# Start-up of a four-part layer kernel: loads from two engines, and batch 0's first steps placed among the set-up

## The chip, the cores and the metric

The kernel runs on one core of one Trainium2 chip. The metric is the device time of one execution in microseconds (us); lower is better. A core has five engines that each run their own list of instructions: PE (matmul, transposes), DVE (vector), ACT (activation), POOL (GpSimd) and SP (here it issues DMAs and nothing else). They meet at semaphores only. Sixteen DMA engines move the data.

## The reference

The input is x of 16 batches by 512 tokens by 128 features, float32. Four blocks follow each other, each closed by a norm:

1. RWKV: `x1 = LN(x)*g0 + b0`; `xn = LN(x1)`; three mixes `xn*mix + shift(xn)*(1-mix)`, where `shift` moves by one token; k, v, r by 128x512 matrices; two recurrences over the tokens, `s = k + decay*s`, where `decay = exp(-exp(tm_decay))`; read-out, residual, then a channel mix (two mixes, silu, sigmoid gate).
2. A soft tree of depth 8: sigmoid gates of `(x Wq) routers^T`, 256 leaf probabilities, times leaf values, times `Wout`, plus a bias.
3. Causal attention of 16 heads of 8 dimensions with rotary positions, after an RMS norm.
4. A mixture of 16 experts with the two best kept, and two shared experts.

Weights are used in forms that the kernel makes itself: `Wq` and the routers are fused, the leaves and `Wout` are fused, the expert matrices are transposed, and the rotary matrices are laid out by dimension.

## The kernel before, in words

**Set-up.** SP issues batch 0's load of x, then 41 loads of weights and vectors in one loop over the list LOADS (L312), every one of them adding to the one semaphore "loaded". The ten short vectors (`pre_g` to `norm_scale`, 128 numbers each, one column of the tile `vec` each) are last in the list. POOL meanwhile fills constants (L326), among them `kh` (75 rows of 8192, the key heads' tile with rows of ones), and makes the identity and the masks (L331). Then every engine waits for the whole of "loaded" (`ALL_LOADED`):

- DVE scales weights (L576 to L581), lays out `w_rope` (L586 to L588), makes the products of vectors `now_g`, `before_g` (L592 to L597), splits the expert biases (`brow_part`, L603 to L613) and the shared bias (`bias_part`, L617 to L629), and, after the fused matmuls, finishes `w_leaf` (L631, L633), which counts "leafed".
- PE waits for "loaded", "scaled", "rot" and "brow_parts", then turns 23 matrices (TURNS: routers, leaves, `wout`, centroids, shared and 16 expert matrices, L852) through the PSUM banks, bank n mod 8, and does the fused matmuls (L855, L857). Before its first batch step it waits for "leafed" and for the bias rows.
- ACT makes `decay` and `first` (L445 to L448), copies each turned matrix out of its bank (L452), and the fused results (L454, L456).
- SP waits for the bias parts, issues three small loads of `bias_rows` (L315), and starts its batch steps.

**Batches.** After the set-up each engine runs the order written out by hand in ORDER. A token `1:mix1` is step mix1 of the batch that lies one turn back. `run` goes through 16 turns and the lags behind; in one turn several batches are at work in different blocks. The first steps of a batch form one chain: `moments0` (DVE, L643 and L648) of x0, `root0` (POOL, L341 to L349), `norm0` (ACT, L469), `x1_gain` and `x1_bias` (POOL, L366, L370), `moments1` (DVE), `root1` (POOL), `norm1` (ACT) into `hat`, `xnT` (PE, L867, four transposes into T0, which is bank 0), `mix_before0` to 2 (ACT, L463), `mix0` to 2 (DVE, L652) into `mixed`, and then `k0` (PE, L871), the first matmul with `wk`, which waits for all three mixes. The DVE order of the next turn begins with mix1, mix2 and `moments0` of the next batch, then `clamp0`. In SP's order, step `load` in turn 0 loads x of batch 1.

The shortest statement of what orders a turn (L276 to L279):

```python
for turn in range(B + max(lag for lag, _ in order)):
    for lag, name in order:
        if 0 <= turn - lag < B:
            steps[name](turn - lag)
```

Of the kernel before, what the change touches and what calls it, by code (L numbers as in the profile page):

```python
# [21 lines left out]
DH = 8  # L22
# [71 lines left out]
def build(nc: bass.Bass, a, out):  # L94
    with ExitStack() as ctx:
        def sb(name, shape, dt=F32):
# [4 lines left out]
                 ("loaded", "brow_parts", "zeroed", "ident", "scaled", "decay1", "decay", "turned_ps", "turned", "fused_ps", "fused", "leafed",  # L101
# [131 lines left out]
        def value_columns(j, g, q):  # L233
# [5 lines left out]

        LOADS = [  # L240
# [6 lines left out]
            (g0[:, :], a["L0_attn_ln0_g"].rearrange("(o h) -> o h", o=1).broadcast_to([P, P])),  # L247
            (b0[:, :], a["L0_attn_ln0_b"].rearrange("(o h) -> o h", o=1).broadcast_to([P, P])),
# [24 lines left out]
        def run(engine, steps):  # L273
# [13 lines left out]
        def _(sp):  # L287
# [33 lines left out]
        def _(pool):  # L321
            zeroed = (ident[:, :], identb[:, :], maskb[:, :], maskTb[:, :], vaug[:, :], ksum[:, :, 0:1], kvsum[:, 0:1],
                      gT[:, :], owner[:, :], brow_part[:, :, :], bias_rows[:, :], max_cols[:, :], gate_cols[:, :])
            filled = ((exponent[:, :], -0.5), (minus_one[:, :], -1.0), (eps_ln[:, :], LN_EPS), (keps[:, :], K_EPS), (kh[:, :, :], 1.0), (ones_rows[:, :], 1.0))
# [106 lines left out]
            pool.wait_ge(setup["loaded"], ALL_LOADED)  # L431
            run("pool", {
# [5 lines left out]
            })  # L438
# [3 lines left out]
        def _(act):  # L442
            act.wait_ge(setup["loaded"], ALL_LOADED)
            act.wait_ge(setup["ident"], 6)
            act.activation(dec_e[:, :], tdec[:, :], ACT.Exp).then_inc(setup["decay1"], 1)  # L445
            act.activation(first[:, :], tfirst[:, :], ACT.Exp).then_inc(setup["decay1"], 1)
            act.wait_ge(setup["decay1"], 2)
            act.activation(decay[:, :], dec_e[:, :], ACT.Exp, scale=-1.0).then_inc(setup["decay"], 1)  # L448

            for n, (_, rows, dst) in enumerate(TURNS):  # L450
                act.wait_ge(setup["turned_ps"], n + 1)
                act.activation(dst, bank[n % 8][:, 0:rows], ACT.Copy).then_inc(setup["turned"], 1)  # L452
            act.wait_ge(setup["fused_ps"], 1)
# [724 lines left out]
```

## Time and profile before

| | |
|---|---|
| median of 3 runs | 1983.46 us (1978.99 to 1986.34) |
| the profiled execution's own time | 1981.15 us |
| its span in the trace | 1979.4 us |
| busy share of the span: PE, DVE, ACT, POOL | 84%, 77%, 51%, 46% |
| granted TensorE clock, mean over the span | 0.944 of full |

The profile is of one execution. Its span runs from the first to the last instruction. "PE" is a matmul's time, "PEld" a weight load, "SPq" the SP queue that issues DMAs. PEclk is the TensorE clock that was granted, as a share of full speed (1.00 is 2.4 GHz, 0.50 is 1.2 GHz). A line such as L643 is that of the kernel's source.

### The profile page before, as it was taken

Reading aid. Unit: us, or ns where it says so; the run is one execution under the profiler, and the core shown is the slowest. Engines: PE = TensorE matmul, PEld = TensorE weight load, DVE = VectorE, ACT = ScalarE, POOL = GpSimd, SP = SyncE. Lnnn points to the kernel's source line nnn. Section 1 sums busy time; section 2 is a strip of 40 time slices with the busy share of each in tenths; the row PEclk is TensorE's granted clock in tenths of the full one; section 3 lists DMA queues with packets and bytes.
Section 4 is the critical chain, followed back from the end, with each engine's and each line's share of the span. In section 5 each row is a group of like instructions: output and inputs, shape, how many; then the busy total and the mean of one; then the engine's idle time right before and its main releaser. Section 6 shows DMA issues by size and latency. Waiting matters only on the chain.

```text
span 1979.4 us, 33699 instructions
## 1 busy us (share of the span) xinstructions
PE 1664.5 (84%) x12063; PEld 1082.8 (55%) x12141; DVE 1526.5 (77%) x3386; ACT 1005.9 (51%) x1997; POOL 914.3 (46%) x1117
## 2 busy tenths in 40 slices
PE   1365799989898999989898989989898989988785
PEld 1133456565565656565565656565665657564535
DVE  2756879889797979889797979789797969783712
ACT  1232374655646374655556474746556464736252
POOL 3436253635545363635455364636355463622202
PEclk9677899999999999999999999999999999999887
DMA  3001010010101010010101010100101010100000
GB/s 97 0 6 48 7 39 17 8 54 8 54 8 49 7 54 6 24 37 8 54 7 49 7 54 7 37 25 8 54 8 54 2 54 2 45 11 25 31 7 6
DMA packets 64617, 53.35 MB, mean 27 GB/s; under 512 B 6018, under 2 KB 63170, under 8 KB 64450
## 3 DMA queue, kind: packets, MB, share of 16 engines
q1 hardware_dynamic: 64450, 51.19, 8.4%
q8 instruction: 97, 1.59, 0.4%
q14 instruction: 70, 0.57, 0.1%
HBM read 8.44 MB, written 4.19 MB: 6 GB/s over the span
## 4 chain that ended last, share of the span: by engine, by line
PE 42%; DVE 36%; issue 6%; ACT 5%; SPq 5%; POOL 3%; DMA 3%; DVEq 0%; ACTq 0%; POOLq 0%
PE bank L871 40%; DVE rmax L742 12%; SPq L300 4%; DVE rmax L739 3%; DVE wkb L689 3%; ACT prob L463 3%; DVE prob L822 3%; PE bank L867 3%; DMA kh<-part 2%; DVE stats L643 2%; DVE tree L652 1%; DVE kvsum L681 1%; DVE kk L665 1%; SPq L312 1%; DVE ksum L676 1%
## 5 line engine op out<-in xcount | busy, mean ns | idle before, releaser
L463 ACT ACTIVATE prob<-bank 128x512 f32<-128x512 f32 x640 | 359.4, 600 | 85.6 <-PE bank L871 80.1
L742 DVE TENSOR_REDUCE rmax<-bank 128x1 f32<-128x512 f32 (+2 forms) x768 | 353.4, 504 | 29.6 <-PE bank L871 29.1
L871 PE MATMUL bank<-kh,qh 72*128 72x512 bf16 (+3 forms) x1024 | 259.8, 308 | 52.8 <-DVE rmax L742 38.1
L871 PE MATMUL bank<-qh,kh 75*128 75x512 bf16 (+3 forms) x1024 | 257.4, 306 | 24.7 <-ACT prob L463 20.8
L871 PE MATMUL bank<-wexpT,prob 128*128 128x128 f32 x2048 | 271.7, 280 | 2.1 <-POOL prob L429 0.6
L871 PEld LDWEIGHTS bank<-wexpT,prob 128*128 128x128 f32 x2048 | 258.7, 195 | 21.0 <-issue 15.9
L429 POOL TENSOR_TENSOR prob<-xdT,spread 128x512 f32<-128x512 f32 x128 | 173.6, 1356 | 193.5 <-ACT spread L463 193.4
L463 ACT ACTIVATE spread<-bank 128x512 f32<-128x512 f32 x128 | 76.5, 597 | 298.1 <-PE bank L871 251.1
L871 PEld LDWEIGHTS bank<-qh,kh 75*128 75x128 bf16 x1024 | 100.1, 98 | 205.4 <-ACT prob L463 146.0
L689 DVE RECIPROCAL wkb<-wkb 128x512 f32<-128x512 f32 x64 | 211.6, 3326 | 0.0
L871 PE MATMUL bank<-maskb,identb 128*128 128x128 bf16 x1024 | 194.3, 223 | 0.0
L871 PE MATMUL bank<-maskTb,identb 128*128 128x128 bf16 x1024 | 192.9, 221 | 0.0
L871 PEld LDWEIGHTS bank<-kh,qh 72*128 72x128 bf16 x1024 | 102.1, 100 | 140.0 <-DVE rmax L742 78.7
L871 PE MATMUL bank<-prob,vaug 128*32 128x512 f32 (+3 forms) x2048 | 173.9, 446 | 0.0
L341 POOL TENSOR_TENSOR var<-mv,eps_ln 128x4 f32<-128x4 f32 x112 | 27.8, 248 | 271.3 <-DVE mv L648 270.6
L463 ACT ACTIVATE rth<-bank 128x512 f32<-128x512 f32 x128 | 75.1, 592 | 150.7 <-PE bank L871 137.3
L375 POOL TENSOR_TENSOR wkb<-wkb,ksum 128x512 f32<-128x512 f32 x64 | 77.2, 1213 | 129.8 <-DVE ksum L676 117.7
L871 PE MATMUL bank<-mixed,cwk 128*128 128x512 f32 x128 | 87.8, 803 | 43.4 <-DVE mixed L652 43.4
L871 PEld LDWEIGHTS bank<-maskb,identb 128*128 128x128 bf16 x1024 | 102.6, 100 | 37.8 <-issue 25.7
L871 PEld LDWEIGHTS bank<-maskTb,identb 128*128 128x128 bf16 x1024 | 101.4, 99 | 25.8 <-issue 25.0
L384 POOL TENSOR_TENSOR rth<-rth,kvb 128x512 f32<-128x512 f32 x64 | 96.9, 1515 | 39.2 <-DVE kvb L652 39.2
L345 POOL TENSOR_TENSOR rstd<-var,exponent 128x4 f32<-128x4 f32 x112 | 113.6, 1014 | 1.2
(209 smaller groups left out, 3401.6 us busy)
## 6 DMA issues: line engine op xcount, KB each, us to landing
qh<-part SPq DMA_DIRECT2D x144, 128.0 KB
kh<-part SPq DMA_DIRECT2D x144, 128.0 KB
x<-in_L_attn_x_dram SPq DMA_DIRECT2D x16, 256.0 KB, 2.9
out_dram<-yo SPq DMA_DIRECT2D x16, 256.0 KB, 2.3
qh<-maxT SPq DMA_DIRECT2D x16, 48.0 KB
wk<-in_L_attn_tm_Wk_dram SPq DMA_DIRECT2D x1, 256.0 KB
wv<-in_L_attn_tm_Wv_dram SPq DMA_DIRECT2D x1, 256.0 KB
wr<-in_L_attn_tm_Wr_dram SPq DMA_DIRECT2D x1, 256.0 KB
```

Source lines behind the costliest of these rows:

```text
L300: sp.dma_start(dst[r:KROWS:PARTS * PARTS, :, :], part[t][m][:, :]).then_inc(sems["heads_in"], 16)
L345: raised(pool.tensor_tensor(rstd[:, n, :], var[:, n, :], exponent[:, :], ALU.pow), f"root{n}")
L375: raised(pool.tensor_tensor(wkb[:, c % 2, :], wkb[:, c % 2, :], ksum[:, c % 2, 0:T], ALU.add), "wk")
L384: raised(pool.tensor_tensor(rth[:, c % 2, :], rth[:, c % 2, :], kvb[:, c % 2, :], ALU.mult), "gated")
L429: raised(pool.tensor_tensor(ug[:, e % 4, :], xdT[:, :], spread[e // 2 % 2][:, :], ALU.mult), "ug_side")
L463: raised(act.activation(dst, src, func, **kw), signal)
L689: raised(dve.reciprocal(wkb[:, c % 2, :], wkb[:, c % 2, :]), "wk_inv")
L739: last = dve.tensor_reduce(rmax[:, 1, h:h + 2], S[n % 2].rearrange("p (h s) -> p h s", h=2), AX_X, ALU.max)
L742: last = dve.tensor_reduce(rmax[:, j, h:h + 1], S[n % 2][:, col:col + (j + 1) * P], AX_X, ALU.max)
L822: raised(dve.tensor_tensor(ug[:, e % 4, :], xdT[:, :], G, ALU.mult), "ug")
L867: last = pe.transpose(bk[:, j * P:(j + 1) * P], t[:, j, :], ident[:, :])
L871: return pe.matmul(out_, w, x, start=start, stop=stop, **kw)
```

## The change

The loads are split over two issuing engines. SP issues x of batch 0, the two gains `g0` and `b0` (semaphore "first_loaded"), and every second entry of the list of 29 remaining loads (15 of them). ACT issues the ten vectors (also "first_loaded") and the other 14. Batch 0's steps up to `mix2` are taken out of the ordered run and placed among the set-up steps, by hand, on each engine: DVE makes the vectors' products and `moments0` before it waits for "loaded", and `moments1` after `w_rope`; POOL does root0, x1_gain, x1_bias, root1 before it waits for "loaded"; ACT does `norm0` before "loaded", `norm1` and `mix_before0` to 2 between the 7th and 8th of its copies of turned matrices; PE does `xnT` between its 14th and 15th transposes. The turned matrices go through banks 1 to 7, since bank 0 takes `xnT`. PE no longer waits for "rot" and "brow_parts" ahead of the transposes but behind the fused matmuls, and for "scaled" at the 7th of them. The fill of `kh` moves on POOL from the constants to behind root1, with a semaphore of its own ("kh_ones"), and SP waits for that ahead of its batch steps. The bodies of all steps, and the order of all later batches, are the same.

The diff, cut to its core (the DVE step functions only move ahead of the set-up code; they are left out):

```diff
+        FIRST = [(v_[n], a[src].rearrange("(p o) -> p o", o=1)) for n, src in
...
+        GAINS = [(g0[:, :], a["L0_attn_ln0_g"].rearrange("(o h) -> o h", o=1).broadcast_to([P, P])),
+                 (b0[:, :], a["L0_attn_ln0_b"].rearrange("(o h) -> o h", o=1).broadcast_to([P, P]))]
...
+        ALL_FIRST = 16 * (len(FIRST) + len(GAINS))
         ALL_LOADED = 16 * len(LOADS)
...
+        def run(engine, steps, begun=()):
...
                 for lag, name in order:
+                    if turn == lag and name in begun:
+                        continue
                     if 0 <= turn - lag < B:
                         steps[name](turn - lag)
+
+        BEGUN = dict(pool=("root0", "x1_gain", "x1_bias", "root1"), act=("norm0", "norm1", "mix_before0", "mix_before1", "mix_before2"),
+                     dve=("moments0", "moments1", "mix0", "mix1", "mix2"), pe=("xnT",))
...
             load(0)
-            for dst, src in LOADS:
+            for dst, src in GAINS:
+                sp.dma_start(dst, src, allow_slow_non_contiguous=True).then_inc(setup["first_loaded"], 16)
+            for dst, src in LOADS[0::2]:
                 sp.dma_start(dst, src, allow_slow_non_contiguous=True).then_inc(setup["loaded"], 16)
             sp.wait_ge(setup["bias_parts"], 7)
             for i in range(PARTS):
                 sp.dma_start(bias_rows[i:i + 1, :], bias_part[i]).then_inc(setup["bias_in"], 16)
+            sp.wait_ge(setup["kh_ones"], 1)
...
-            pool.wait_ge(setup["loaded"], ALL_LOADED)
-            run("pool", {
...
+            pool.wait_ge(setup["first_loaded"], ALL_FIRST)
+            for name in BEGUN["pool"]:
+                pool_steps[name](0)
+            pool.memset(kh[:, :, :], 1.0).then_inc(setup["kh_ones"], 1)
+            pool.wait_ge(setup["loaded"], ALL_LOADED)
+            pool.wait_ge(setup["kh_ones"], 1)
+            run("pool", pool_steps, BEGUN["pool"])
...
         @block.scalar
         def _(act):
...
+            for dst, src in FIRST:
+                act.dma_start(dst, src, allow_slow_non_contiguous=True).then_inc(setup["first_loaded"], 16)
+            for dst, src in LOADS[1::2]:
+                act.dma_start(dst, src, allow_slow_non_contiguous=True).then_inc(setup["loaded"], 16)
...
+            def take_turns(a, z):
+                for n in range(a, z):
+                    _, rows, dst = TURNS[n]
+                    act.wait_ge(setup["turned_ps"], n + 1)
+                    act.activation(dst, bank[1 + n % 7][:, 0:rows], ACT.Copy).then_inc(setup["turned"], 1)
+
+            act.wait_ge(setup["first_loaded"], ALL_FIRST)
+            act.wait_ge(setup["ident"], 6)
+            turns["norm0"](0)
+            act.wait_ge(setup["loaded"], ALL_LOADED)
...
+            take_turns(0, 7)
+            turns["norm1"](0)
+            act.wait_ge(setup["mix_g"], 2)
+            for name in BEGUN["act"][2:]:
+                turns[name](0)
+            take_turns(7, len(TURNS))
...
         @block.vector
         def _(dve):
...
+            dve.wait_ge(setup["first_loaded"], ALL_FIRST)
             for i, (m, ln) in enumerate(MIXES):
...
+            dve.wait_ge(setup["mix_g"], 2)
+            dve_steps["moments0"](0)
+            dve.wait_ge(setup["loaded"], ALL_LOADED)
...
             last.then_inc(setup["rot"], 1)
 
+            dve_steps["moments1"](0)
             def after_steps(n):
...
             dve.tensor_tensor(bias_part[2], bias_rest, bias_part[1], ALU.subtract).then_inc(setup["bias_parts"], 1)
+            for name in BEGUN["dve"][2:]:
+                dve_steps[name](0)
             dve.wait_ge(setup["fused"], 2)
...
         @block.tensor
         def _(pe):
             pe.wait_ge(setup["ident"], 6)
             pe.wait_ge(setup["loaded"], ALL_LOADED)
-            pe.wait_ge(setup["scaled"], 6)
-            pe.wait_ge(setup["rot"], 1)
-            pe.wait_ge(setup["brow_parts"], 6)
             for n, (src, rows, _) in enumerate(TURNS):
-                if n >= 8:
-                    pe.wait_ge(setup["turned"], n - 7)
-                pe.transpose(bank[n % 8][:, 0:rows], src, ident[0:rows, 0:rows]).then_inc(setup["turned_ps"], 1)
+                if n == 6:
+                    pe.wait_ge(setup["scaled"], 6)
+                if n == 14:
+                    pe_steps["xnT"](0)
+                if n >= 7:
+                    pe.wait_ge(setup["turned"], n - 6)
+                pe.transpose(bank[1 + n % 7][:, 0:rows], src, ident[0:rows, 0:rows]).then_inc(setup["turned_ps"], 1)
             pe.wait_ge(setup["turned"], len(TURNS))
...
+            pe.wait_ge(setup["rot"], 1)
+            pe.wait_ge(setup["brow_parts"], 6)
             pe.wait_ge(setup["fused"], 2)
             pe.wait_ge(setup["leafed"], 2)
             pe.wait_ge(setup["bias_parts"], 7)
             pe.wait_ge(setup["bias_in"], 16 * PARTS)
+            run("pe", pe_steps, BEGUN["pe"])
```

## Rows read from the trace of the kernel before

**Rows 1.** The page, part 4: the chain that ended last, by engine.
```profile
PE 42%; DVE 36%; issue 6%; ACT 5%; SPq 5%; POOL 3%; DMA 3%; DVEq 0%; ACTq 0%; POOLq 0%
```

**Rows 2.** Busy time by stretches (us busy, xcount; last three: clock, DMA share, GB/s).
```profile
0.00:10.00 10.00, 0.00 (x0) 0.00 (x0) 0.00 (x0) 0.00 (x0) 9.47 (x22) 1.00 0.70 197
10.00:20.00 10.00, 0.00 (x0) 0.00 (x0) 0.00 (x0) 1.28 (x1) 3.57 (x8) 1.00 0.55 148
20.00:28.50 8.50, 0.00 (x0) 0.00 (x0) 0.00 (x0) 0.00 (x0) 0.00 (x0) 1.00 0.52 125
60.00:1979.40 1919.40, 1656.24 (x12030) 1076.05 (x12106) 1512.86 (x3321) 993.00 (x1957) 895.67 (x1078) 0.95 0.08 25
```

**Rows 3.** The same view in steps of 1 us, while the loads run.
```profile
7.00:8.00 1.00, 0.00 (x0) 0.00 (x0) 0.00 (x0) 0.00 (x0) 1.00 (x1) 1.00 1.11 318
...
13.00:14.00 1.00, 0.00 (x0) 0.00 (x0) 0.00 (x0) 0.11 (x1) 0.81 (x5) 1.00 0.09 27
...
26.00:27.00 1.00, 0.00 (x0) 0.00 (x0) 0.00 (x0) 0.00 (x0) 0.00 (x0) 1.00 0.14 1
```

**Rows 4.** Timeline of SP's queue: start, us it took to issue, what.
```profile
0.72 0.45 SPq L291 DMA_DIRECT2D x<-in_L_attn_x_dram  x1
...
10.82 2.43 SPq L312 DMA_DIRECT2D prob<-n_L_ffn_leaf_values_dram  x1
...
18.30 3.02 SPq L312 DMA_DIRECT2D prob<-in_L_ffn_br_dram  x3
...
22.60 0.43 SPq L312 DMA_DIRECT2D vec<-in_L_attn_pre_b_dram  x1
...
38.64 0.58 SPq L291 DMA_DIRECT2D x<-in_L_attn_x_dram  x1
```

**Rows 5.** Timeline of the set-up after the loads: start, us, what, [idle before <-releaser].
```profile
28.57 0.43 DVE L576 TENSOR_SCALAR cwv<-cwv 128x512 f32<-128x512 f32 x1 [28.57 <-DMA vec<-n_L_attn_norm_scale_dram]
...
30.84 0.15 DVE L592 TENSOR_TENSOR now_g<-vec 128x1 f32<-128x1 f32 x1
...
31.93 0.21 DVE L603 CAST brow_part<-prob 48x128 bf16<-48x128 f32 x1
...
33.58 5.33 PE L852 MATMUL bank<-ident,prob 128*128 128x128 f32 x23 [33.58 <-DVE owner L613]
...
35.74 3.48 ACT L452 ACTIVATE wexpT<-bank 128x128 f32<-128x128 f32 x16
35.97 0.68 DVE L629 TENSOR_TENSOR part<-kk,part 1x512 bf16<-1x512 f32 x1
...
39.28 0.71 PE L855 MATMUL bank<-prob 128*128 128x255 f32 x2 [0.37 <-ACT wexpT L452]
...
39.82 0.61 PE L857 MATMUL bank<-prob 128*128 128x128 f32 x4
...
41.34 0.29 DVE L633 TENSOR_SCALAR w_leaf<-w_leaf 128x256 f32<-128x256 f32 x1
```

**Rows 6.** Timeline of batch 0's first steps, in the same form.
```profile
41.55 0.87 DVE L643 BATCH_NORM_STATS2 stats<-x 128x6 f32<-128x128 f32 x4
...
44.73 1.65 ACT L469 ACTIVATE x<-x,shift,rstd 128x128 f32<-128x128 f32 x4 [3.88 <-POOL shift L349]
46.45 1.26 POOL L366 TENSOR_TENSOR x<-x,g 128x512 f32<-128x512 f32 x1 [1.84 <-ACT x L469]
...
49.09 0.87 DVE L643 BATCH_NORM_STATS2 stats<-x 128x6 f32<-128x128 f32 x4 [6.26 <-POOL x L370]
...
55.00 2.12 ACT L463 ACTIVATE mix_part<-bank,vec,before_g 128x511 f32<-128x511 f32 x3 [1.27 <-PE bank L867]
...
59.27 1.22 PE L871 MATMUL bank<-mixed,wk 128*128 128x512 f32 x1 [4.31 <-DVE mixed L652]
```

**Rows 7.** Timeline of POOL: the fill of kh, and one form of L379 twice.
```profile
5.22 6.92 POOL L326 MEMSET kh<- 75x8192 bf16 x1
...
65.37 1.52 POOL L379 TENSOR_SCALAR rth<-rth 128x512 f32<-128x512 f32 x1
...
70.37 0.62 POOL L379 TENSOR_SCALAR rth<-rth 128x512 f32<-128x512 f32 x1
```

**Rows 8.** Busy time by stretches, around PE's pause (columns as in group 2).
```profile
42.00:45.00 3.00, 0.00 (x0) 0.00 (x0) 0.79 (x7) 0.27 (x1) 1.52 (x4) 0.62 0.01 3
```

More of the change, by code:

```diff
@@ L100, in build @@
         setup = {n: ctx.enter_context(nc.semaphore(f"w_{n}")) for n in
-                 ("loaded", "brow_parts", "zeroed", "ident", "scaled", "decay1", "decay", "turned_ps", "turned", "fused_ps", "fused", "leafed",
+                 ("first_loaded", "loaded", "kh_ones", "brow_parts", "zeroed", "ident", "scaled", "decay1", "decay", "turned_ps", "turned", "fused_ps", "fused", "leafed",
                   "rot", "bias_parts", "bias_in", "mix_g")}
@@ L581, in _ @@
-            dve.tensor_scalar(wshs, wshs, 0.5, None, ALU.mult).then_inc(setup["scaled"], 1)
-            half = DH // 2
-            for t, w in enumerate((aq, ak)):
-                by_dim = w[:, :].rearrange("p (h d) -> p d h", d=DH)
-                dve.tensor_copy(w_rope[:, 2 * t, :, :], by_dim)
-                dve.tensor_scalar(w_rope[:, 2 * t + 1, 0:half, :], by_dim[:, half:DH, :], -1.0, None, ALU.mult)
-                last = dve.tensor_copy(w_rope[:, 2 * t + 1, half:DH, :], by_dim[:, 0:half, :])
@@ new lines, in _ @@
+            for i, (m, ln) in enumerate(MIXES):
+                last = dve.tensor_tensor(before_g[:, i:i + 1], v_[ln + "_g"], now_g[:, i:i + 1], ALU.subtract)
+            last.then_inc(setup["mix_g"], 1)
+            dve.wait_ge(setup["mix_g"], 2)
+            dve_steps["moments0"](0)
+            dve.wait_ge(setup["loaded"], ALL_LOADED)
+            dve.tensor_scalar(cwv[:, :, :], cwv[:, :, :], 0.5, None, ALU.mult).then_inc(setup["scaled"], 1)
+            dve.tensor_tensor(wshs, wsh[:, 0, :], wsh[:, 1, :], ALU.add).then_inc(setup["scaled"], 1)
@@ new lines, in _ @@
+            for w in (aq, ak, av):
+                dve.tensor_scalar(w[:, :], w[:, :], v_["norm_scale"], None, ALU.mult).then_inc(setup["scaled"], 1)
+            dve.wait_ge(setup["scaled"], 5)
+            dve.tensor_scalar(wshs, wshs, 0.5, None, ALU.mult).then_inc(setup["scaled"], 1)
+            half = DH // 2
+            for t, w in enumerate((aq, ak)):
+                by_dim = w[:, :].rearrange("p (h d) -> p d h", d=DH)
+                dve.tensor_copy(w_rope[:, 2 * t, :, :], by_dim)
+                dve.tensor_scalar(w_rope[:, 2 * t + 1, 0:half, :], by_dim[:, half:DH, :], -1.0, None, ALU.mult)
+                last = dve.tensor_copy(w_rope[:, 2 * t + 1, half:DH, :], by_dim[:, 0:half, :])
@@ L842, in _ @@
+            dve.wait_ge(setup["rot"], 1)
+            run("dve", dve_steps, BEGUN["dve"])
         @block.tensor
         def _(pe):
[L844 to L852 removed]
@@ L853, in _ @@
-            pe.wait_ge(setup["turned"], len(TURNS))
-            pe.matmul(bank[0][:, 0:NODES], tq, routersT[:, 0:NODES], start=True, stop=True).then_inc(setup["fused_ps"], 1)
-            for k in range(2):
-                last = pe.matmul(bank[1][:, k * P:(k + 1) * P], leavesT[:, k * P:(k + 1) * P], woutT, start=True, stop=True)
-            last.then_inc(setup["fused_ps"], 1)
-            pe.wait_ge(setup["fused"], 2)
-            pe.wait_ge(setup["leafed"], 2)
-            pe.wait_ge(setup["bias_parts"], 7)
@@ L1143, in _ @@
                 "gT": turn_gates, "shared": start_experts, "biases": expert_biases, **each("gb", NE, spread_gate), **each("expert", NE, expert),
-            })
+            }
+            pe.wait_ge(setup["ident"], 6)
+            pe.wait_ge(setup["loaded"], ALL_LOADED)
+            for n, (src, rows, _) in enumerate(TURNS):
+                if n == 6:
[5 more added lines that the diff above has]
+                pe.transpose(bank[1 + n % 7][:, 0:rows], src, ident[0:rows, 0:rows]).then_inc(setup["turned_ps"], 1)
+            pe.wait_ge(setup["turned"], len(TURNS))
+            pe.matmul(bank[1][:, 0:NODES], tq, routersT[:, 0:NODES], start=True, stop=True).then_inc(setup["fused_ps"], 1)
+            for k in range(2):
+                last = pe.matmul(bank[2][:, k * P:(k + 1) * P], leavesT[:, k * P:(k + 1) * P], woutT, start=True, stop=True)
+            last.then_inc(setup["fused_ps"], 1)
+            pe.wait_ge(setup["rot"], 1)
+            pe.wait_ge(setup["brow_parts"], 6)
+            pe.wait_ge(setup["fused"], 2)
+            pe.wait_ge(setup["leafed"], 2)
+            pe.wait_ge(setup["bias_parts"], 7)
+            pe.wait_ge(setup["bias_in"], 16 * PARTS)
+            run("pe", pe_steps, BEGUN["pe"])
 _UNUSED = ["L0_ffn_leaf_keys"]
```

144 lines of the change are left out of this document (60 added, 84 removed).

## The prediction

> **What bounds the kernel now.** I read the chain of waits first [rows 1]. PE and DVE make up 78% of it: that is the steady work of the batches, and the change leaves it alone. The change can touch only what lies ahead of it, so I read the busy time by stretches next [rows 2]. Before 28.5 us PE, DVE and ACT do practically nothing: the loads bound this part. Then the timelines show two things in series: set-up work of the four engines from 28.57 to 41.6 us [rows 5], and batch 0's first steps, from moments0 at 41.55 to the first matmul k0 at 59.27 us, in which most of the time one engine works and the others wait [rows 6]. From there each engine follows its written order, and every later wait is on a semaphore of another step. Nothing there is tied to the clock on the wall, so k0's start is the handle: what it moves forward, the end moves forward, as far as the clock of TensorE does not differ. Hence I work out k0's new start. Call L the moment at which all loads have landed; now it is 28.55.
>
> **Part 1, the loads.** The DMA engines are busy 0.70, 0.55 and 0.52 of the three stretches, which is 10 x 0.70 + 10 x 0.55 + 8.5 x 0.52 = 16.9 us of all sixteen engines [rows 2]. In single microseconds the share is 1.11 at 7 us, but 0.09 at 13 us, where SP is held at one load for 2.43 us, and 0.14 at 26 us, where only short vectors go out [rows 3, 4]. So SP's issuing and the order of the list cost 28.5 - 16.9 = 11.6 us beyond the bare transfers. A plain issue takes 0.43 us and starts about 0.47 behind the last; held ones take up to 2.43 [rows 4]. ACT's price for an issue is nowhere in this trace. Its bounds: SP's 0.43 us below (nothing excludes less, but that would gain little, as the transfers bind next) and 2.43 above; I take 0.47 each, SP's pace, since these are the same kinds of loads. ACT has 24: 0.7 + 24 x 0.47 = 12.0 us, plus its half of SP's held time. SP's 42 issues ended at 26.8, so the held time was 26.8 - 0.7 - 42 x 0.47 = 6.4 us; the entries that cause most of it (the odd half of the routers ahead of the 2.43, the expert matrices ahead of the biases' 3.02 for three) both fall to ACT, so I give it 5 us. ACT is then free at about 17. SP has 18 issues and ends at 11 to 13. The transfers need 16.9 us behind a start at 2, and the last ones (1 MB of experts, shared experts) are issued at 14 to 17 us: they can land at 19 to 21. The ideal is 18.9; I take **L = 21**, a gain of 7.5 us.
>
> Here stands a rule against the change. The rows just named show the DMA engines half idle because the issuer was late or held. The Trainium skill (DMA: Bandwidth & Descriptors, "Issuing engines are not separate DMA queues") says that issuing from several engines saves only the sequencer's time, usually small beside the transfer. By that rule alone L would stay near 28.5; the shares of 0.09 and 0.14 say that here the issuer's time is not small. It is rival A.
>
> **Part 2, what runs ahead of L.** first_loaded needs x, the two gains and ten vectors, the last issued at about 5.4, landed at 8 (a vector took 2.2 us from its issue at 26.39 to DVE's start at 28.57). moments0 and root0 fit between 9 and 12. POOL is free, as the 6.92 us fill of kh [rows 7] has moved. norm0 cannot start before ACT has issued its loads: 17, and if the table load of 1.28 us (ACT's one instruction in [rows 2]) comes behind the issues, 18.3. Then 1.65 for norm0 and 2.6 for gain and bias (46.45 to 49.09, [rows 6]): x1 is ready at 22.7. DVE asks for it after its weight scaling and w_rope, 2.3 us behind L (28.57 to 30.84, [rows 5]), at 23.3. So this costs nothing by 0.6 us of cover; each microsecond that ACT is later than that goes into the sum in full.
>
> **Part 3, the chain behind L.** From moments1's start to mix_before's end it took 57.12 - 49.09 = 8.0 us [rows 6]; none of its work has changed: 23.3 + 8.0 = 31.3. The first 14 transposes, seven copies and DVE's bias work (31.93 to 36.65, 4.7 us, [rows 5]) lie beside it: DVE ends moments1 at 24.6 and the bias work at 29.3, below 31.3. If that cover went, DVE's three mixes would come later, and they have until leafed. ACT now makes its last 16 copies behind mix_before: 3.5 us [rows 5], to 34.8. From there the way to leafed is as before: 39.22 to 41.6, 2.4 us: 37.2. DVE's mixes (2.1 us) are ready at 33.4, beside it. PE stood still from about L + 3 to norm1's end. Before, a pause like that brought its clock down from 1.00, 0.62 in the mean of the 3 us after it, and then 0.50, that is 1.2 GHz [rows 8]; at that level the fused matmuls' 0.71 + 0.61 us double, +1.3. I take half: **k0 starts at about 38**, against 59.27. Gain 21.3 us, of which 7.5 is L and 13.8 the overlap (59.27 - 28.55 = 30.7 behind L before, 17 now).
>
> **Part 4, what was added to SP and POOL.** POOL fills kh behind root1: moments1 ends at 24.6, root1 at 26.2, the fill at 33.1. SP's three bias loads end near 31.3, so kh_ones is what holds it; behind it stands the load of batch 1, issue 0.58 [rows 4] and about 3 us to land: 36.8. DVE wants that x for moments0 of batch 1, which stands ahead of clamp0. It has until about 1 us behind k0's start, 39, so the wait costs nothing with 2 us of cover. The fill ran beside an idle DVE; now DVE is at work. One POOL form took 0.62 us once and 1.52 beside a DVE scan [rows 7]. By that ratio, 2.45, taken as the upper end, the fill takes 17.0 us and the load lands at 46.9: 8 us lost. By the lower end it takes 6.92. DVE's work beside it is bias pieces on few partitions and three mixes, not scans, so I take 6.92 to 8 and no loss. The heads' DMAs, which need the ones, come much later.
>
> **Sum.** 1981.15 (this execution's own time, 1.75 above its span) - 21.3 = 1959.9. The median of the runs is 2.3 above this execution, so the forecast for a median is **1962 us**, 1.1% faster. About 0.5%, 10 us, is what can be told from no change, as the three runs spread over 7.4 us.
>
> **Rivals.**
> A. *The two queues do not overlap* (shared transfers or a shared generator of descriptors): L stays 28.5. For it: the peak shares of 1.11 show that in the dense stretches the engines are full, and the list's bytes are the same. Against it: the idle stretches above. Then only 13.8 is gained: 1983.5 - 13.8 = 1970. Chance 0.12.
> B. *The slack on ACT or SP is gone*: issuing from ACT at about 0.9 us each makes it 10 us later, norm0 at 27 to 28, moments1 at 33.4 where 23.3 stood, k0 at 48; or the fill of kh as in part 4. Gain 11 to 13: about 1972. For it: covers of 0.6 and 2 us only. Against it: SP's plain pace. Chance 0.12.
> C. *The gain is lost later, in TensorE's clock*: the batches' clock averages 0.95 from 60 us on [rows 2]; another phase against it could take 1 point of 1656 us PE-busy, 17 us, and leave 1979, no change. Against it: the same work in the same order behind k0. Chance 0.06.
> D. *Slower*: ACT's issues cost the 2.43 us of the longest SP issue. Then they end at 0.7 + 24 x 2.43 = 59, norm0 runs there, and k0 follows 59 + 1.65 + 2.6 + 8.0 + 3.5 + 2.4 = 77, 18 us later than now: 2001. It decides from (59.27 - 18.2 - 0.7) / 24 = 1.7 us an issue. SP showed such a time only where a load before it was awkward. Chance 0.03.
> E. *The change does not do what it says*, because the skipped steps or the order hide another wait (the ones in kh late for the heads, say): no more than the start is at stake, 1975 to 1985. Chance 0.03.
> The forecast itself: 0.64.
>
> **How the numbers follow.** Low end: L at 18.9 and the clock full behind the transposes, 3 us better, and 3 for the spread of the runs: 1956. High end: A and B with the spread: 1974. Faster by over 0.5% is the forecast, A and most of B: 0.89. Within: C, E and some of B, 0.08. Slower: 0.03.
>
> **What would show it.** DMA shares of 0.8 and above from 3 to 19 us, DVE's cwv at 20 to 22; one x1 normed by ACT at 17 to 19 with no wait of DVE for it of over 1 us; 16 copies behind mix_before; k0 at 37 to 39; DVE's moments0 of batch 1 not waiting for its DMA. From k0 to the end 1920 us as before, within 4. Wrong: cwv behind 26, an ACT issue over 0.7 us on the mean, or k0 early and the end not.

## The result, and the profile after

| | before | changed |
|---|---|---|
| median of 15 runs each | 1982.8 us | 1971.3 us (1964.68 to 1979.7) |
| ratio, 95% interval | | 0.9944 (0.9929 to 0.9958) |
| the profiled execution's own time, its span | 1981.15, 1979.4 | 1969.9, 1968.1 us |
| last load landed (start of DVE's `cwv`) | 28.57 us | 25.37 us |
| k0 starts | 59.27 us | 45.27 us |
| first `clamp` starts | 61.38 us | 48.36 us |

The kernel is 0.56% faster: 11.1 us by the ratio, with an interval of 8.3 to 14.1. The forecast was 21. The two profiled executions differ by 11.3 us in span: k0 starts 14.0 us earlier, and 2.7 of these are gone again by the end.

First the busy time by stretches of the changed kernel, in the columns of [rows 2]:

```profile
0.00:10.00 10.00, 0.00 (x0) 0.00 (x0) 0.00 (x0) 0.00 (x0) 6.19 (x28) 1.00 0.53 126
10.00:20.00 10.00, 0.00 (x0) 0.00 (x0) 2.44 (x23) 0.16 (x1) 1.52 (x4) 1.00 0.75 211
20.00:28.50 8.50, 1.51 (x6) 1.10 (x6) 3.09 (x7) 4.69 (x14) 2.59 (x2) 1.00 0.46 134
```

The DMA share fell in the first stretch (0.53, where it was 0.70) and rose in the second (0.75, where it was 0.55). Vectors first means few bytes first: the ten vectors are 0.5 KB each. The loads end 3.2 us earlier, not 7.5. The timeline of the changed kernel says why, and what came after (start, us, what, [idle before <-releaser]; "SPq" and "ACTq" rows are issues):

```profile
3.61 1.71 ACTq L459 DMA_DIRECT2D vec<-in_L_attn_post_b_dram  x1
3.69 1.66 SPq L320 DMA_DIRECT2D cwv<-in_L_attn_cm_Wv_dram  x1
...
12.57 3.78 ACTq L461 DMA_DIRECT2D prob<-in_L_attn_Wq_dram  x1
...
13.29 0.16 DVE L806 TENSOR_TENSOR now_g<-vec 128x1 f32<-128x1 f32 x1 [13.29 <-DMA vec<-n_L_attn_norm_scale_dram]
...
18.95 2.23 ACTq L461 DMA_DIRECT2D prob<-in_L_ffn_br_dram  x1
21.21 0.45 ACTq L461 DMA_DIRECT2D prob<-in_L_ffn_Ws_dram  x1
21.77 1.28 ACT L471 ACT_TABLE_LOAD   x1 [3.74 <-issue]
...
24.79 1.27 POOL L375 TENSOR_TENSOR x<-x,g 128x512 f32<-128x512 f32 x1 [7.21 <-ACT x L471]
...
25.37 0.97 DVE L817 TENSOR_SCALAR cwv<-cwv 128x512 f32<-128x512 f32 x1 [9.57 <-DMA prob<-in_L_ffn_Ws_dram]
...
26.26 1.35 DVE L818 TENSOR_TENSOR prob<-prob 128x128 f32<-128x128 f32 x1
...
32.18 7.01 DVE L852 TENSOR_SCALAR wkb<-wkb 1x128 f32<-1x128 f32 x1
32.19 6.92 POOL L450 MEMSET kh<- 75x8192 bf16 x1
...
35.21 2.11 ACT L465 ACTIVATE mix_part<-bank,vec,before_g 128x511 f32<-128x511 f32 x3 [1.27 <-PE bank L879]
...
41.90 2.05 DVE L616 SCALAR_TENSOR_TENSOR mixed<-bank,now_g,mix_part 128x512 f32<-128x512 f32 x3
...
43.95 0.59 SPq L297 DMA_DIRECT2D x<-in_L_attn_x_dram  x1
...
45.27 2.04 PE L883 MATMUL bank<-mixed,wk 128*128 128x512 f32 x2 [3.10 <-DMA bias_rows<-part]
...
47.16 0.87 DVE L607 BATCH_NORM_STATS2 stats<-x 128x6 f32<-128x128 f32 x4 [2.56 <-DMA x<-in_L_attn_x_dram]
```

Four things are to be seen. ACT is held at issues (3.78, 2.23, 1.71 us) and is free only at 21.66: 24 issues in 20.9 us, 0.87 us each on the mean, though a plain one follows the last by 0.48, much like SP's 0.47. DVE's first two set-up steps take 0.97 and 1.35 us beside POOL's gain and bias, where they took 0.43 [rows 5] and 0.29. A multiply of 1 by 128 numbers (L852), 0.21 us in the kernel before, takes 7.01 us: it starts and ends with POOL's fill of `kh`. And k0's releaser is no longer a mix but the bias rows' DMA, which hang on that multiply; the x of batch 1, issued behind them, holds DVE once more at 47.1.

### The profile page after: what moved, and what is told of

Same layout as the page of the kernel before. It is cut to its first block, busy times and chain, and to the rows that moved or that the text cites. A ratio compares the mean times of both kernels' runs of the same rounds, so it can differ in the third digit from the quotient of the medians.

```text
span 1968.1 us, 33778 instructions
## 1 busy us (share of the span) xinstructions
PE 1674.3 (85%) x12141; PEld 1082.3 (55%) x12141; DVE 1535.9 (78%) x3386; ACT 1005.6 (51%) x1998; POOL 915.5 (47%) x1117
## 4 chain that ended last, share of the span: by engine, by line
PE 51%; DVE 29%; ACT 5%; issue 5%; SPq 3%; POOL 3%; DMA 3%; ACTq 1%; DVEq 0%; POOLq 0%
PE bank L883 48%; DVE rmax L706 9%; SPq L306 3%; DVE wkb L653 3%; ACT prob L465 3%; PE bank L879 3%; DVE prob L786 2%; DVE rmax L703 2%; DMA kh<-part 2%; DVE tree L616 1%; DVE stats L607 1%; DVE inner L616 1%; DVE kk L629 1%; DVE hot L770 1%; ACT hat L471 1%
## 5 line engine op out<-in xcount | busy, mean ns | idle before, releaser
L883 PEld LDWEIGHTS bank<-wexpT,prob 128*128 128x128 f32 x2048 | 258.0, 194 | 20.8 <-issue 15.9
L883 PE MATMUL bank<-gT,owner 128*128 128x512 bf16 x256 | 98.2, 384 | 19.8 <-DVE prob L786 16.1
```

Of the source, the lines that this page charges most:

```text
L883: return pe.matmul(out_, w, x, start=start, stop=stop, **kw)
```

## The experiments

Theory T: the end moves with k0; k0 stands at the loads' end plus a fixed chain, plus what the new overlaps cost. Its rivals are with each run. All starts below are from one profiled execution each (the timeline); "gain" is against the kernel before. The median of the kernel before was 1981.6 to 1985.5 us in the rounds beside the experiments, so the last column is what can be compared between kernels, and the medians only roughly.

| kernel | `cwv` | k0 | first clamp | median, us | ratio (95%) |
|---|---|---|---|---|---|
| before | 28.57 | 59.27 | 61.38 | | 1 |
| changed | 25.37 | 45.27 | 48.36 | 1971.3 | 0.9944 (0.9929 to 0.9958) |
| e1_one_queue | 27.98 | 46.28 | 49.46 | 1971.4 | 0.9945 (0.9918 to 0.9971) |
| e2_two_queues_only | 25.30 | 55.79 | 57.90 | 1977.4 | 0.9972 (0.9952 to 0.9992) |
| e3_kh_early | 25.48 | 43.79 | 45.87 | 1969.7 | 0.9921 (0.9895 to 0.9948) |
| e4_kh_in_pieces | 25.53 | 43.83 | 45.91 | one run | |
| e5_routers_split | 23.66 | 40.37 | 42.45 | one run | |
| e11_small_fixes_timed (e5 again) | 23.73 | 40.43 | 42.51 | 1966.5 | 0.9908 (0.9873 to 0.9943) |
| e7_loads_balanced | 24.04 | 40.47 | 41.60 | 1969.9 | 0.9917 (0.9879 to 0.9954) |
| e6_chain_ahead | 24.38 | 33.79 | 39.89 | 1968.8 | 0.9931 (0.9906 to 0.9955) |
| e8_x1_load_first | 24.60 | 34.13 | 35.77 | 1960.7 | 0.9884 (0.9839 to 0.9930) |
| e12_best_timed (e8 again) | 24.22 | 33.70 | 35.34 | 1962.9 | 0.9894 (0.9864 to 0.9924) |
| e9_pe_filler | 24.30 | 34.42 | 35.73 | 1965.7 | 0.9897 (0.9864 to 0.9931) |
| e10_change_again | 25.84 | 45.73 | 48.81 | one run | |

### Which half of the change gave the gain: e1 and e2

```diff
 (e1: the changed kernel, all loads on SP)
+            for dst, src in GAINS + FIRST:   ... first_loaded
+            for dst, src in LOADS:           ... loaded
-            act.dma_start(...) for FIRST and LOADS[1::2]
```

> The changed kernel with every load issued by SP again (x, the two gains, the ten vectors, then the other 29), the interleaving kept. Theory T (the end moves with k0, and k0 is set by the last load's landing L plus a fixed chain): L goes from 25.4 back to about 28.5, and k0 from 45.3 to 47 to 48.5 (less than 3.1 later where POOL's gain and bias no longer lie beside DVE's first set-up steps, since ACT is free for norm0 early); time about 1974, 9 us under the kernel before. Rival Q (the second queue brings nothing, as all loads share the same sixteen DMA engines): L and k0 stay at 25.4 and 45.3, time 1971.

```diff
 (e2: the kernel before, loads split as in the change, all on "loaded")
+        others = LOADS[:9] + LOADS[11:31]
+        SP_LOADS, ACT_LOADS = LOADS[9:11] + others[0::2], LOADS[31:] + others[1::2]
```

> The kernel before with its loads split over SP and ACT in the same order as the change, and nothing else (kh filled early, batch 0's steps behind the set-up). Theory T: L at 25.4, the old 30.7 us behind it, k0 at 56, time 3 us under the kernel before (1979.5), so most of the change's gain is the interleaving. Rival: the gain of the change is mostly the queues, and this kernel has most of the 11.5 us: 1973.

Two rows of the timeline of e1_one_queue:

```profile
27.98 0.43 DVE L813 TENSOR_SCALAR cwv<-cwv 128x512 f32<-128x512 f32 x1 [15.18 <-DMA wkb<-in_L_ffn_bs_dram]
...
46.28 2.05 PE L879 MATMUL bank<-mixed,wk 128*128 128x512 f32 x2 [3.11 <-DMA bias_rows<-part]
```

And two of e2_two_queues_only:

```profile
25.30 0.43 DVE L581 TENSOR_SCALAR cwv<-cwv 128x512 f32<-128x512 f32 x1 [25.30 <-DMA prob<-in_L_ffn_Ws_dram]
...
55.79 2.07 PE L876 MATMUL bank<-mixed,wk 128*128 128x512 f32 x2 [4.31 <-DVE mixed L657]
```

With one queue the interleaving alone moves k0 by 59.27 - 46.28 = 13.0 us. The two queues alone move it by 3.5. Together they give 14.0: on top of the interleaving the second queue is worth 1.0 us at k0, though the loads end 2.6 earlier (27.98 against 25.37). The other 1.6 us is what DVE's first steps lose in the change (3.9 us for 2.3): in e1 ACT issues nothing, norm0 is done at 17.6, and they run beside an idle POOL. Theory T gave 47 to 48.5 for k0 in e1, which came 0.7 us ahead of that, and 56 in e2, which held. Rival Q fails on the loads' end, yet is nearly right on the outcome: the ratios of e1 and of the change are 0.9945 and 0.9944. A difference of 1 us is below what they can tell (e1's interval is 5.8 to 16.3 us); that it is 1 us is read at k0 alone.

### What held DVE for 7 us: e3 and e4

```diff
 (e3)
             pool.wait_ge(setup["ident"], 6)
+            pool.memset(kh[:, :, :], 1.0).then_inc(setup["kh_ones"], 1)
...
-            pool.memset(kh[:, :, :], 1.0).then_inc(setup["kh_ones"], 1)   (behind root1)
```

> The changed kernel with the 6.9 us fill of kh put back early on POOL (behind the identity and masks, where POOL waits from 7 to 16 us and DVE is idle). Theory P (DVE's 1x128 multiply of the shared bias at 32.2 us took 7.0 us because POOL's fill held the SBUF port that it needs, for the whole instruction): it takes 0.2 us, the bias rows are in by 39, k0 waits for leafed and starts at about 43.3 where it was 45.3, batch 1's x has landed by then, the first clamp starts at about 45.5 instead of 48.4, and the end comes about 3 us earlier (1968.5). Rival S (the DVE instruction is slow for a reason of its own, or POOL's fill does not matter at k0): the multiply still takes over 2 us, k0 at 45, time 1971.

```diff
 (e4: in the change's place)
-            pool.memset(kh[:, :, :], 1.0).then_inc(setup["kh_ones"], 1)
+            for k in range(8):
+                pool.memset(kh[:, k * (NH // 8):(k + 1) * (NH // 8), :], 1.0).then_inc(setup["kh_ones"], 1)
 (SP and POOL then wait for 8 of "kh_ones")
```

> The changed kernel with the fill of kh in the same place but as eight memsets of two heads each (0.87 us each). Theory P, a lock held for an instruction: DVE gets in between pieces, no bias instruction waits much over 0.9 us, and DVE's bias steps (L850 to L862 of the changed kernel, 10.1 us there, 3.3 us in the kernel before) take 3.5 to 7 us in all; k0 at 43.3 to 44.5. Rival W (POOL's writes slow DVE in proportion as long as they go on, whatever the size of an instruction): the bias steps still take about 10 us, k0 at 45.3.

The timeline of e3_kh_early:

```profile
7.02 6.92 POOL L346 MEMSET kh<- 75x8192 bf16 x1
...
32.29 0.21 DVE L852 TENSOR_SCALAR wkb<-wkb 1x128 f32<-1x128 f32 x1
...
43.79 2.04 PE L883 MATMUL bank<-mixed,wk 128*128 128x512 f32 x2 [1.52 <-issue]
```

And DVE and POOL in that of e4_kh_in_pieces:

```profile
32.32 1.93 DVE L853 TENSOR_SCALAR wkb<-wkb 1x128 f32<-1x128 f32 x1
32.34 8.10 POOL L451 MEMSET kh<- 75x1024 bf16 x8
...
34.28 1.13 DVE L855 COPY kk<-wkb 1x512 f32<-1x512 f32 x1
35.45 1.13 DVE L857 CAST part<-kk 1x512 bf16<-1x512 f32 x1
36.61 0.68 DVE L859 TENSOR_TENSOR kk<-kk,part 1x512 f32<-1x512 f32 x1
37.33 0.42 DVE L861 CAST part<-kk 1x512 bf16<-1x512 f32 x1
```

Moved to where DVE is idle, the fill costs DVE nothing: 0.21 us for the multiply, k0 at 43.79, the clamp 2.5 us earlier than in the change. (At the end, 0.9921 against 0.9944 fits that, but the intervals overlap.) In eight pieces the multiply takes 1.93 us, the copy and the first cast 1.13 each (0.41 in the kernel before), while the subtraction with two inputs takes its usual 0.68. A second cast, at 37.33, takes 0.42: not every one beside the pieces is held. The bias steps take 6.4 us in all, where one piece of fill took them to 10.1 and none is 3.3. So the wait goes with the size of POOL's instruction and with DVE's kind of instruction, which is theory P and not rival W: POOL fills even longer (8.1 us), and by rival W the steps would have stayed at 10. The Trainium skill (SBUF — State Buffer, "Who interferes with whom") says just this: a shared pair of ports is held for a whole instruction and the loser blocks; it names copies, casts and multiplies with a scalar as DVE's side, and says that an operation with two inputs contends only with a POOL operation that reads. The traces agree on each: the subtraction beside a fill (which only writes) kept its time, and `wshs` (L818, two inputs) beside POOL's bias addition (which reads) took 1.35 us. One point is neither in the Trainium skill nor in theory P, which had no wait much over 0.9: the first multiply took as long as two pieces (of 1.0 us each), not one. Why was not tried.

### What set the loads' end: e5, e7 and e11

```diff
 (e5, on e3)
-            (routers[0:NODES - P, 1, :], a["L0_ffn_routers"][P:NODES, :]),
+            (routers[0:112, 1, :], a["L0_ffn_routers"][P:P + 112, :]),
+            (routers[112:NODES - P, 1, :], a["L0_ffn_routers"][P + 112:NODES, :]),
 (the entries behind it change sides between SP and ACT)
```

> The kernel with kh filled early, and the load of the routers' last 127 rows made of two loads, 112 and 15 rows (one more issue on the list, so the entries behind it change sides). Theory R (a load of 127 rows runs on one DMA engine, its ring fills, and ACT's next issue, Wq of the attention, is held for 3.78 us): the next issue takes about 0.5 us, ACT's last issue ends at 18 instead of 21.7, L comes at 22 instead of 25.4 and k0 at 40.5 instead of 43.8. Rival (the hold is from the number of bytes or descriptors under way, whatever their engines): some later issue is held instead, L stays at 25, k0 at 43.8.

```diff
 (e7, on e5)
+        EASY = (1, 3, 5, 6, 20, 21)
+        ON_ACT = [LOADS[k] for k in EASY]
+        ON_SP = [load for k, load in enumerate(LOADS) if k not in EASY]
+            SP: x, GAINS + FIRST[6:], ON_SP      ACT: FIRST[:6], ON_ACT
```

> As the kernel with the routers' load split and kh early, but ACT issues six of the vectors and six large plain loads only (wv, cwk, wo, cwv and the two rotary tables), and SP all the rest (x, gains, four vectors, 24 loads). ACT is free at about 8 us, so norm0 and the gain and bias lie well ahead of L. Theory T: L = about 21 (SP: 31 issues of 0.47 and about 3 us of holds end at 18.5, plus 2.5 to land), DVE's first set-up steps take 2.3 us again instead of 3.9 as POOL's gain and bias are over, k0 at L + 16.5 = 38. Rival (the sixteen DMA engines bind, with a share near 1 from 3 us on): L at 23 to 25, k0 at 40 to 42.

> The kernel with kh filled early and the routers' load split, timed in rounds. Its k0 repeats at 40.4, 18.9 us ahead of the kernel before and 4.9 ahead of the changed one. Theory T (the end moves with k0): median ratio to the kernel before 0.9905 (18.9 us), that is about 1963 to 1965. Rival: the gain behind the changed kernel's is lost on the way, ratio 0.994 as the changed kernel.

The timeline of e5_routers_split:

```profile
11.85 4.82 SPq L320 DMA_DIRECT2D prob<-in_L_ffn_br_dram  x1
11.97 0.86 ACTq L461 DMA_DIRECT2D prob<-n_L_ffn_leaf_values_dram  x1
...
17.52 1.28 ACT L471 ACT_TABLE_LOAD   x1 [17.52 <-POOL shift L359]
...
40.37 2.05 PE L883 MATMUL bank<-mixed,wk 128*128 128x512 f32 x2 [1.52 <-issue]
```

That of e7_loads_balanced, issues first:

```profile
5.04 1.50 ACTq L464 DMA_DIRECT2D cwv<-in_L_attn_cm_Wv_dram  x1
5.09 1.46 SPq L323 DMA_DIRECT2D cwr<-in_L_attn_cm_Wr_dram  x1
6.57 1.65 ACTq L464 DMA_DIRECT2D cos_t<-in_rope_cos_dram  x1
6.60 1.63 SPq L323 DMA_DIRECT2D tdec<-in_L_attn_tm_decay_dram  x1
...
24.04 0.43 DVE L820 TENSOR_SCALAR cwv<-cwv 128x512 f32<-128x512 f32 x1 [10.77 <-DMA wkb<-in_L_ffn_bs_dram]
```

Busy time by stretches: first of the changed kernel, then of e5_routers_split, then of e7_loads_balanced.

```profile
12.00:16.00 4.00, 0.00 (x0) 0.00 (x0) 2.44 (x23) 0.00 (x0) 0.01 (x1) 1.00 1.05 304
16.00:21.00 5.00, 0.00 (x0) 0.00 (x0) 0.00 (x0) 0.16 (x1) 1.51 (x4) 1.00 0.59 168
```

```profile
12.00:21.00 9.00, 0.00 (x0) 0.00 (x0) 2.44 (x23) 2.93 (x5) 3.92 (x6) 1.00 1.11 308
```

```profile
0.00:10.00 10.00, 0.00 (x0) 0.00 (x0) 0.00 (x0) 0.00 (x0) 9.17 (x29) 1.00 0.36 76
6.00:8.00 2.00, 0.00 (x0) 0.00 (x0) 0.00 (x0) 0.00 (x0) 1.94 (x6) 1.00 0.21 4
10.00:20.00 10.00, 0.00 (x0) 0.00 (x0) 2.44 (x23) 2.93 (x5) 6.72 (x7) 1.00 1.10 297
```

Theory R named the hold, and it went: behind the split load the next issue took 0.86 us where it was 3.78 in the change and 2.82 in e3, and ACT was free at 16.9 instead of 21.7. In e5 that next issue is another load than in e3. A fairer pair is on SP alone: the leaf values, issued right behind the routers, took 2.43 us in the kernel before [rows 4] and 1.51 in e1, but 0.47 in e7, where the routers' load is split. The Trainium skill (DMA: Bandwidth & Descriptors, "Why a DMA increments its semaphore by 16 and not by 1") says that a load of 127 rows runs on one engine and one of 128 on sixteen, and its rule gives sixteen for 112 rows too; the hold and its end agree, though no trace here shows which engine a load ran on. But L came at 23.7, not 22, and another hold grew on SP: 4.82 us behind the expert matrices. That is the rival's picture, for half the amount. That k0 came at 40.4, near theory R's 40.5, is in part luck: L was 1.7 us later than in the theory, and the theory had not counted that POOL's gain and bias would lie ahead of L and DVE's first steps be short again (1.6 us).

Neither long hold kept the DMA engines idle while it lasted. In the change the share was 1.05 from 12 to 16 us, with ACT held, and fell to 0.59 from 16 to 21, when SP had no loads left and ACT's last six went out one by one. In e5 it stayed at 1.11 from 12 to 21. As far as the shares show, then, e5 gained at L because the rest of the list was no longer left to one late queue; the split and the new sides of the entries behind it were not tried apart.

Balancing (e7) then brought no earlier end: 24.04. From 10 to 20 us the sixteen DMA engines have a share of 1.10 in the sum of their packets' times. The rival of e7 (share near 1, L at 23 to 25, k0 at 40 to 42) holds in its numbers, but the engines are full only from about 10 us on: over the first ten the share is 0.36. SP and ACT are held together there and let go together (5.04 and 5.09, 6.57 and 6.60; in the change 3.61 and 3.69), and with both held from 6 to 8 us the share is 0.21. So part of a hold is shared by both queues and is not made by full engines. What it is was not tried; nor was a list for both queues with large loads ahead of the vectors.

Timed, e11 gives 0.9908, about 18 us (11 to 25), by k0's 18.8: theory T; the rival's 0.994 lies at the edge of its interval.

### How far it goes: e6, e8, e12 and e9

```diff
 (e6, on e7)
-            pool.memset(kh[:, :, :], 1.0).then_inc(setup["kh_ones"], 1)
+            dve.memset(kh[:, :, :], 1.0).then_inc(setup["kh_ones"], 1)      (DVE, first)
             dve_steps["moments0"](0)
+            dve_steps["moments1"](0)
             dve.wait_ge(setup["loaded"], ALL_LOADED)
...
+            act.activation(scratch[:, :], vec[:, 0:1], ACT.Exp)
             turns["norm0"](0)
+            turns["norm1"](0)
             act.wait_ge(setup["loaded"], ALL_LOADED)
             (decay, first)
+            mix_before0 to 2, then take_turns(0, len(TURNS))
...
             pe.wait_ge(setup["ident"], 6)
+            pe_steps["xnT"](0)
             pe.wait_ge(setup["loaded"], ALL_LOADED)
 (leafed is waited for in leaf_sum(0), the bias rows in start_experts(0); DVE: mixes ahead of the bias parts)
```

> All together, as a version to beat both: the loads as in the balanced kernel; DVE fills kh before the first loads land; moments1, norm1, xnT and the mixes stand ahead of the wait for all loads or right behind it instead of between the transposes; a first small exponential of ACT pulls its table load out of the chain; PE waits for leafed and the bias rows only where it uses them. Theory T: the chain of batch 0 ends (mixes) at about 28, the 23 copies and the fused matmuls at 29 to 31, k0 starts at 30 to 33, 12 to 15 us ahead of the changed kernel, and the time is 1957 to 1960. Rival (a start earlier by that much is given back, since the batches' own waits or TensorE's clock absorb it): the time stays at 1965 to 1971.

```diff
 (e8, on e6)
+            load(1)
             sp.wait_ge(setup["bias_parts"], 7)
 (the step load of turn 0 then issues nothing)
```

> The kernel with batch 0's chain ahead of the loads' end, and the load of x for batch 1 issued by SP before it waits for the bias parts. Theory L (with k0 at 33.8, DVE's moments0 of batch 1 waited until 38.7 for that load, and the first clamp stood behind it at 39.9): the clamp starts at 36, the first output is stored some 3 us earlier than in that kernel (gain of 20 to 21 us at the first store against the kernel before). Rival: the clamp is held by something else (K's matmul at the lower clock) and starts at 38 or later.

> The fastest version so far (batch 0's chain ahead of the loads' end, balanced loads, kh filled by DVE, x of batch 1 issued early) in five more rounds. Theory T (the end moves with k0, 25 us ahead of the kernel before, give or take a few us of TensorE's clock): ratio 0.987 to 0.990. Rival: the four runs of before were lucky and the ratio is that of the two small fixes, 0.991 or above.

```diff
 (e9, on e8; its filler's results are never read)
+                        if engine == "pe" and turn <= 1:
+                            steps["filler"](0)
+            def filler(b):
+                for _ in range(8):
+                    mm(S[0][:, 0:P], ones_rows[:, :], maskTb[:, :])
```

> The same kernel, with eight small matmuls (128x128, bf16, on constants, into a bank that nothing uses yet, their result never read) ahead of every PE step of the first two turns. Theory C (the early kernels give back part of what k0 gained because TensorE's granted clock was 0.50 over 40 to 50 us, so that K's matmul pair took 1.91 us where 1.02 is to be had): the granted clock is 1.00 in most of 35 to 100 us, and the first store comes 3 to 6 us earlier than without the filler (gain 24 to 27). Rival F (the filler's own time, about 0.5 to 0.9 us ahead of each of some 20 waits, eats what the clock gives): first store within 1 us or later.

The timeline of e6_chain_ahead:

```profile
2.49 6.88 DVE L806 MEMSET kh<- 75x8192 bf16 x1 [2.49 <-issue]
...
33.79 1.10 PE L887 MATMUL bank<-mixed,wk 128*128 128x512 f32 x2 [0.68 <-ACT w_leaf L596]
...
38.69 0.87 DVE L609 BATCH_NORM_STATS2 stats<-x 128x6 f32<-128x128 f32 x4 [4.37 <-DMA x<-in_L_attn_x_dram]
```

Its busy time from 40 us on, and below it the same stretch of e8_x1_load_first:

```profile
40.00:50.00 10.00, 7.93 (x8) 2.18 (x8) 8.17 (x7) 2.80 (x5) 5.50 (x7) 0.50 0.00 1
```

```profile
40.00:50.00 10.00, 7.66 (x14) 2.04 (x12) 9.27 (x8) 3.46 (x6) 6.94 (x9) 0.86 0.00 0
```

e6 brought k0 to 33.8, just behind the 30 to 33 expected, but of its further 6.7 us against e7 nothing arrived at the end: 0.9931 and 1968.8 us, where 1957 to 1960 was expected. The rival, a gain given back behind k0, came true. The trace shows two leaks. DVE waited 4.37 us for batch 1's x, so the clamp gained 21.5 where k0 gained 25.5. And PE, idle meanwhile, was granted 1.2 GHz through 40 to 50 us. Issuing that load early (e8) put the clamp at 35.8 and the granted clock to 0.86 in the stretch; the first output is stored 23.2 us earlier than in the kernel before (e6: 17.4), and the time is 0.9884 and, in a second set of runs (e12), 0.9894. That is the fastest version: by the ratios 21 us under the kernel before, 10 under the change. The intervals of e6 and e12 still touch (0.9906 to 0.9955, 0.9864 to 0.9924).

How much of e6's loss is the clock is not shown. In e8 the low clock came later, not never: 0.65 and 0.50 from 50 to 60 and 60 to 70 us, where e6 has 0.56 and 0.78. The filler of e9 did raise the granted clock (1.00 from 30 to 50 us), but its first store came 6 us later than e8's, where theory C had 3 to 6 earlier, and the time is no better (0.9897). That is rival F's outcome; that it was the filler's own time is argued only.

### How far a single trace can be trusted behind k0: e10

> The changed kernel once more, for a second trace of the same program. Theory N (what lies between k0 and the end differs by several us between executions, from TensorE's clock alone): up to the first clamp every time repeats within 0.5 us (cwv at 25.4, k0 at 45.3), while k0 to the end, 1922.8 us in the first trace, differs by 2 to 8 us. Rival: it repeats within 1 us, so the differences between kernels behind k0 are the kernels' own.

The same program once more: `cwv` 0.47 us later, k0 at 45.73, and 1968.5 - 45.73 = 1922.8 us from there to the end, as the first time (1968.1 - 45.27). The expected difference at the end was not there. It was there on the way: the tenth output is stored 14.0 us ahead of the kernel before in one trace and 9.9 in the other, the thirteenth 14.7 and 9.7. The two traces of e5 and e11, one program, have k0 at 40.37 and 40.43, and spans of 1959.8 and 1963.8. And e2's profiled execution ended 3.8 us later than that of the kernel before, with k0 3.5 earlier. So differences of 5 us and more behind k0 in one trace are no property of a kernel; the 15 executions of the change alone lie between 1964.7 and 1979.7 us.

The end is therefore read from the ratios. Gain at the end for gain at k0, in us: e2 5.6 (1.6 to 9.5) for 3.5, e1 10.9 (5.8 to 16.3) for 13.0, the change 11.1 (8.3 to 14.1) for 14.0, e3 15.7 (10.3 to 20.8) for 15.5, e11 18.3 (11.3 to 25.2) for 18.8, e7 16.4 (9.1 to 24.0) for 18.8, e12 21.0 (15.1 to 27.0) for 25.6: theory T holds within the intervals. It fails in e6, 13.7 (8.9 to 18.6) for 25.5, and there even the clamp's 21.5 lies outside.

## Why the prediction was right or wrong

**Right.** The sign, the range (1956 to 1974), "faster by over 0.5%", and the mechanism in outline: the loads' end and the interleaving moved k0, and k0 the end. From k0 to the end it took 1922.8 us (1920.1 before), inside the 4 us allowed.

**How near it was.** The gain is about half of the 21 forecast. The measured 0.56% has an interval of 0.42 to 0.71, so "over 0.5%" held narrowly, and 1971.3 lies in the part of the range that was there for rivals A and B. Of the prediction's own signs, "k0 at 37 to 39", "cwv at 20 to 22", "DMA shares of 0.8 and above from 3 to 19 us" and "moments0 of batch 1 not waiting for its DMA" (it waited 2.56 us) all failed, and one sign of being wrong was met: an ACT issue of 0.87 us on the mean, over the 0.7 named.

**Where the 7.3 us went.** k0 was put at 38 and came at 45.27. By the steps of the sum, with e3 for what the fill of `kh` hides:

| step | predicted | measured | difference |
|---|---|---|---|
| L | 21 | 25.37 | +4.4 |
| DVE's first set-up steps | 2.3 | 29.25 - 25.37 = 3.9 | +1.6 |
| moments1 to mix_before's end | 8.0 | 37.32 - 29.25 = 8.1 | +0.1 |
| 16 copies | 3.5 | 40.04 - 37.32 = 2.7 | -0.8 |
| to k0, without the fill | 3.2 | 43.79 - 40.15 = 3.6 (e3) | +0.4 |
| the fill of `kh` beside DVE | 0 | the rest | +1.6 |

*Part 1, the price of ACT's issue.* This is the step that failed most. A plain issue kept SP's pace, as I took it; what I had wrong is the held time on ACT, 5 us in the sum and 20.9 - 24 x 0.47 = 9.6 in the trace, which made ACT free at 21.7 instead of 17. Rival B had the mean, 0.9 us, at a chance of 0.12. It had not that L would be late with it: the last load to land is ACT's last issue, at 21.2. The even split put the slow entries, the 127-row load and what stands behind the 2048 rows of expert matrices, on ACT; I saw that, and priced them as they stood in a single queue. The rule of the Trainium skill that I set against the trace (DMA: Bandwidth & Descriptors, "Issuing engines are not separate DMA queues"), that issuing from several engines saves only the sequencer's time, was the better guide: the second queue moved L by 2.6 us in the interleaved kernel and by 3.3 alone (e2), and was worth 1.0 us at k0 in the first. The idle stretches before were real. e5 and e7 filled them behind 10 us, with L at 23.7 to 24; the first ten us, at 0.53 and 0.36, stayed half idle or more, where I had 0.8 from 3 us on.

*Part 2.* The vectors landed later than I had them: DVE starts on them at 13.29 and not at 8 (`norm_scale` took 7.0 us from issue to landing, not 2.2). ACT's issues hid that. x1 was ready at 27.46 and not 22.7, and was asked for at 29.2: cover as foreseen, because L was late as well. But the work was not free. It lay beside DVE's steps and cost them 1.6 us. I had counted only who waits for whom, not that DVE and POOL side by side can block each other.

*Part 4.* I looked at the right instruction and the wrong loser. Both ends I gave (6.92 and 17.0 us) were for POOL's fill. POOL kept its 6.92; DVE stood still. [rows 7] shows a POOL form slowed beside a DVE scan; here DVE was slowed beside POOL, and I had looked only one way. The load of batch 1 was late by its other wait, the bias parts (43.95 instead of 33.1), not by kh_ones; that cost 1 us more at the clamp (gain 13.0 where k0 gained 14.0).

*Part 3* held for the chain itself (8.1 us for 8.0, and 2.7 for the copies' 3.5), but not for the bias work beside it, which the fill drew out to 41.96 where I had 29.3: k0's last wait became the bias rows. The overlap term is best tested by e1, where L hardly moved: 13.0 us at k0, 12.4 of them behind L, against 13.8 in the sum, and the 1.4 that are missing are near the 1.5 us that e3 gets back from the fill. The fear in Part 3, a pause of PE that lowers the clock, was in place: the fused matmuls' first pair took 1.22 us (0.71 in [rows 5]).

**Rivals.** A (L unchanged) is out: 25.4. Its number came nearest, 1970 with 13.8 us at k0 where 14.0 were measured, but by luck: of the 14.0, L is 3.2 and the overlap 10.8. B's number is near as well (1972), and its 0.9 us an issue is right, but not what it makes of it: norm0 came at 23.1, not at 27 to 28, and DVE did not wait for x1 at all. C did not show between the two kernels beyond the 2.7 us, which is inside what one trace can differ by; in e6 a loss behind k0 is shown, its cause only in part. D and E are out.

With e3 and e5 together k0 came at 40.4: 4.9 of the 7.3 us are so accounted for by experiment. The other 2.4 are in the main L, at 23.7 where I had 21.

## What to carry to other kernels

When steps are moved beside other engines' work, go through the pairs that will run side by side, POOL with DVE above all, and ask of each which one will block; a long fill belongs where the other is idle. Before counting on a second issuing engine, ask what the first leaves idle in the DMA engines, and price the held issues on the queue that will have them: here it was worth 2.6 us at the loads' end and 1.0 at the first matmul, and a load of 127 rows went with a hold of 3.8 us. And after each microsecond gained at a stage's start, look at the next load behind it: in e6 a 4.4 us wait for the next batch's x stood behind a chain that had won 6.7.

## What was not expected of the hardware

- A DVE multiply of 128 numbers took 7.01 us beside a POOL memset of 6.92, and 1.93 beside memsets of a mean of 1.0 us.
- SP's and ACT's issues were held at the same moments, for 1 to 2.2 us each, in the kernels that use both queues, with a DMA share of 0.16 (change, 4 to 5 us) and 0.21 (e7, 6 to 8 us) meanwhile.
- The column of the granted clock reads 1.00 from the start to 60 us in the changed kernel, while K's first matmul pair at 45.27 took 2.04 us and the next pair but one, at 49.08, 1.12; in e7 the first pair took 1.10 at 40.47 in a stretch with the same 1.00. Durations are the better witness there.
